# One one-hot compare, two maxima and four gelu buffers in a neighbour turn

## The reference

```python
y = affine(conv1x1(x, fc1_w, fc1_b), fc1_s, fc1_t)
nodes = window_partition(y, 8).reshape(Bw, C, 64).transpose(0, 2, 1)
idx = knn_idx(nodes, 9)                      # cosine distance, top_k
x_j = nodes[idx]; x_i = nodes[:, :, None, :]
feat = concatenate([x_i, x_j - x_i], -1)     # 2C
h = gelu((feat @ ew.T + eb) * es + et)       # 96 channels, exact gelu
h = max(h, axis=2)                           # over the 9 neighbours
x1 = affine(conv1x1(h, fc2_w, fc2_b), fc2_s, fc2_t) + x
```

## Time and profile before

| | |
|---|---|
| median of three runs | 654.57 us |
| span of the profiled execution (first to last instruction) | 650.4 us |
| what lies outside the span, against the median | 4.2 us |
| PE busy | 572.0 us, 88% |
| DVE busy | 500.3 us, 77% |
| ACT busy | 435.5 us, 67% |
| POOL busy | 249.4 us, 38% |
| maxima (L1221), 128 of 1203 ns | 151.7 us |
| one-hots (L1206), 64 of 766 ns | 48.9 us |

### The profile page before, as it was taken

The page is one execution under the profiler, slowest core; times in us unless marked ns, Lnnn a source line. Parts: engine busy times, 40 slices in busy tenths (PEclk is TensorE's granted clock), DMA queues, the critical chain, the costliest instruction groups (busy, mean ns, idle before and its releaser), DMA issues.

```text
span 650.4 us, 12840 instructions
## 1 busy us (share of the span) xinstructions
PE 572.0 (88%) x3404; PEld 339.7 (52%) x3404; DVE 500.3 (77%) x962; ACT 435.5 (67%) x645; POOL 249.4 (38%) x299
## 2 busy tenths in 40 slices
PE   6993699999999999939888899999999999988970
PEld 1232466666666556625545566666665565545530
DVE  2687679999999999947998666666667667655665
ACT  3761379999999999928877555555565655644545
POOL 2650103333333333304857534444444434433310
PEclk9995599999999999969989999999999999989985
DMA  8847655666566656685531222222112222296516
GB/s 218 264 144 213 173 137 132 142 147 146 138 147 145 143 145 139 147 164 127 116 71 36 52 62 50 49 50 51 42 33 59 80 75 80 57 182 128 128 54 194
DMA packets 101605, 75.76 MB, mean 116 GB/s; under 512 B 52738, under 2 KB 84996, under 8 KB 101236
## 3 DMA queue, kind: packets, MB, share of 16 engines
q1 hardware_dynamic: 100804, 71.69, 45.6%
q10 hardware_dynamic: 768, 3.67, 2.2%
HBM read 48.84 MB, written 22.15 MB: 109 GB/s over the span
## 4 chain that ended last, share of the span: by engine, by line
PE 40%; DVE 29%; issue 13%; SPq 6%; DMA 5%; ACT 3%; DVEq 1%; POOL 1%; ACTq 0%; POOLq 0%
DVE hmax L1221 12%; PE pz L703 9%; PE pz L682 7%; DVE onehot L1206 5%; PE pz L697 5%; PE p_edge L703 4%; DVE idx L1197 4%; PE p_edge L682 4%; PE pz L533 3%; PE p_edge L697 2%; DVE val L1189 2%; DMA y_hl<-y_d 2%; PE pz L611 2%; DMA ht<-xh 2%; PE p_keys L525 1%
## 5 line engine op out<-in xcount | busy, mean ns | idle before, releaser
L1221 DVE TENSOR_REDUCE hmax<-gel 96x128 f32<-96x1024 f32 x128 | 151.7, 1203 | 19.3 <-ACT gel L828 19.3
L828 ACT ACTIVATE gel<-pz 96x1024 f32<-96x1024 f32 x128 | 130.4, 1018 | 39.5 <-PE pz L611 27.0
L1098 POOL CAST ht<-h 48x512 fp32r<-48x512 f32 x62 | 37.5, 605 | 148.8 <-DVE h L1332 148.3
L703 PE MATMUL pz<-ht,w_xh 128*112 128x512 f32 x258 | 73.0, 419 | 6.1 <-DMA ht<-xh 6.1
L1100 POOL TENSOR_TENSOR ht<-h,ht 48x512 fp32r<-48x512 f32 x62 | 73.5, 1185 | 5.0
L682 PE MATMUL pz<-xh,w_xh 128*112 128x512 f32 (+1 forms) x258 | 69.5, 406 | 0.8 <-DVE w_xh L1231 0.8
L611 PE MATMUL pz<-onehot,ab_hi 64*96 64x512 f32 x256 | 59.9, 464 | 3.0 <-ACT gel L828 2.4
L703 PEld LDWEIGHTS pz<-ht,w_xh 128*112 128x112 f32 x258 | 42.4, 177 | 33.2 <-issue 19.3
L893 ACT ACTIVATE pz<-c 48x512 f32<-48x512 f32 x43 | 25.7, 597 | 47.9 <-DVE c L1325 47.9
L682 PEld LDWEIGHTS pz<-xh,w_xh 128*112 128x112 f32 x258 | 46.0, 179 | 17.4 <-issue 1.2
L1332 DVE SCALAR_TENSOR_TENSOR h<-tgo,pz 48x512 f32<-48x512 f32 x43 | 29.7, 690 | 30.2 <-ACT pz L893 30.2
(11 more groups left out here) (148 smaller groups left out, 1242.0 us busy)
## 6 DMA issues: line engine op xcount, KB each, us to landing
ib<-idx_d SPq DMA_DIRECT2D x64, 256.0 KB, 4.2
y_d<-y SPq DMA_DIRECT2D x32, 192.0 KB, 3.6
y_hl<-y_d SPq DMA_DIRECT2D x32, 192.0 KB, 4.0
hist_d<-h SPq DMA_DIRECT2D x62, 96.0 KB, 1.9
hp<-hist_d SPq DMA_DIRECT2D x30, 192.0 KB, 2.7
kr<-xn_d SPq DMA_DIRECT2D x32, 98.0 KB
xn_d<-x_in SPq DMA_DIRECT2D x32, 96.0 KB, 2.4
kl<-xn_d SPq DMA_DIRECT2D x32, 96.0 KB
```

The lines of the kernel that those rows point to most:

```text
L703: mm = pe.matmul(gate_banks(k, d)[m][0:TOP, :], w_xh[:, 1, d, m, t], moving(ht, slice(0, P), t), start=False, stop=(t == TAPS - 1))
L828: act.activation(gel[:, t % 2], pz[0:O, 2 * (t % 2):2 * (t % 2) + 2, :], ACT.Gelu) \
L1098: pool.tensor_copy(h_slots(ht, 0, d), columns(h2[0:C, d])).then_inc(S["h_top"], 1)
L1221: dve.tensor_reduce(dst, gel[:, t % 2].rearrange("p w (r c k) -> p w r c k", r=WS, k=KN), AX_X, ALU.max).then_inc(S["maxed"], 1)
```

## The change

DVE compares all 2048 columns of a group in one instruction, and takes one maximum over two gelus (2048 columns) in place of two. The buffer gel has four places, one for each gelu of a group, and gelu t now waits for the maximum over the same half of the group before. The counts that other engines wait for (onehots, maxed) go with this: one one-hot and two maxima to a group. On DVE the order within a turn changes too: the one-hot of the next group comes first, then the first maximum, both parts of the top-k, the second maximum and the self maximum.

```diff
--- before.py
+++ after.py
@@ -137,7 +137,7 @@
                 ab_lo = a("ab_lo", [P, 2, Q, 2, O], F32R)
                 val8 = a("val8", [P, Q, KN], F32)
                 idx = a("idx", [P, 2, Q, KN], U16)
-                gel = a("gel", [O, 2, 2, E8], F32)
+                gel = a("gel", [O, Q, 2, E8], F32)
                 selfg = a("selfg", [O, 2, GN], F32)
                 hmax = a("hmax", [O, 2, GN], F32)
                 ident = a("ident", [P, E8], F32R)
@@ -327,7 +327,7 @@
 
                 sp.wait_ge(S[f"idx_stored{b}"], n * 16 + 16)
                 if later(g, 2):
-                    sp.wait_ge(S["onehots"], g * 2 - 2)
+                    sp.wait_ge(S["onehots"], g - 1)
                 for s in range(2):
                     sp.dma_start(ib[HALF * s:HALF * s + HALF, b],
                                  idx_d[reg(g, 0, 1)].rearrange("o (t s) n k -> s o t (n k)", s=2)[s]
@@ -601,7 +601,7 @@
 
                 if t == 0:
                     pe.wait_ge(S["ab_low"], g + 1)
-                pe.wait_ge(S["onehots"], g * 2 + (t // 2 + 1))
+                pe.wait_ge(S["onehots"], g + 1)
                 if t > 1 or later(g):
                     pe.wait_ge(S["gelus"], g * 4 + (t - 1))
                 for n, (part, which, moving) in enumerate(((ab_hi, 1, onehot[:, b, t]), (ab_lo, 1, onehot[:, b, t]),
@@ -823,9 +823,9 @@
 
             def gelu(g, t):
                 act.wait_ge(S["z_done"], g * 4 + (t + 1))
-                if t >= 2 or later(g):
-                    act.wait_ge(S["maxed"], g * 4 + (t - 1))
-                act.activation(gel[:, t % 2], pz[0:O, 2 * (t % 2):2 * (t % 2) + 2, :], ACT.Gelu) \
+                if later(g):
+                    act.wait_ge(S["maxed"], g * 2 + (t // 2 - 1))
+                act.activation(gel[:, t], pz[0:O, 2 * (t % 2):2 * (t % 2) + 2, :], ACT.Gelu) \
                     .then_inc(S["gelus"], 1)
 
             def fc2_out(g, b, n):
@@ -1071,10 +1071,8 @@
 
                 on(-2, x1_cast)
                 if exists(nth(j, b, 1)[0]):
-                    pool.wait_ge(S["onehots"], nth(j, b, 1)[0] * 2 + 1)
+                    pool.wait_ge(S["onehots"], nth(j, b, 2)[0])
                 on(-2, x1_low_first)
-                if exists(nth(j, b, 1)[0]):
-                    pool.wait_ge(S["onehots"], nth(j, b, 2)[0] * 2)
                 on(-1, residual)
                 on(-2, x1_low_second)
                 if isinstance(j, int) and GROUPS - 6 <= nth(j, b, 0)[0] < GROUPS - 4:
@@ -1197,28 +1195,26 @@
                     ins = dve.max_index(idx[:, b, t], val8[:, t], keys_of[t])
                 ins.then_inc(S["topk_done"], 1)
 
-            def one_hot(g, b, n, half):
-
-                if half == 0:
-                    dve.wait_ge(S["idx_here"], g * 32 + 32)
-                    if later(g, 2):
-                        dve.wait_ge(S["z_done"], g * 4 - 4)
-                dve.tensor_scalar(onehot[:, b, 2 * half:2 * half + 2], ib[:, b, 2 * half:2 * half + 2],
-                                  jcol_sb[:, 0:1], None, ALU.is_equal).then_inc(S["onehots"], 1)
+            def one_hot(g, b, n):
+
+                dve.wait_ge(S["idx_here"], g * 32 + 32)
+                if later(g, 2):
+                    dve.wait_ge(S["z_done"], g * 4 - 4)
+                dve.tensor_scalar(onehot[:, b], ib[:, b], jcol_sb[:, 0:1], None, ALU.is_equal) \
+                    .then_inc(S["onehots"], 1)
 
             def self_max(g, b, n):
 
                 dve.wait_ge(S["self_gel"], g + 1)
-                dve.wait_ge(S["maxed"], g * 4 + 4)
+                dve.wait_ge(S["maxed"], g * 2 + 2)
                 dve.tensor_tensor(hmax[:, b], hmax[:, b], selfg[:, b], ALU.max).then_inc(S["self_maxed"], 1)
 
-            def maxima(g, b, n, t):
-                dve.wait_ge(S["gelus"], g * 4 + (t + 1))
-                if t == 0 and later(g, 2):
+            def maxima(g, b, n, h):
+                dve.wait_ge(S["gelus"], g * 4 + (2 * h + 2))
+                if h == 0 and later(g, 2):
                     dve.wait_ge(S["fc2_done"], g - 1)
-                dst = hmax[:, b, HG * (t // 2):HG * (t // 2) + HG] \
-                    .rearrange("p (r w c) -> p w r c", r=WS, c=WS)[:, 2 * (t % 2):2 * (t % 2) + 2]
-                dve.tensor_reduce(dst, gel[:, t % 2].rearrange("p w (r c k) -> p w r c k", r=WS, k=KN),
+                dst = hmax[:, b, HG * h:HG * h + HG].rearrange("p (r w c) -> p w r c", r=WS, c=WS)
+                dve.tensor_reduce(dst, gel[:, 2 * h:2 * h + 2].rearrange("p t w (r c k) -> p (t w) r c k", r=WS, k=KN),
                                   AX_X, ALU.max).then_inc(S["maxed"], 1)
 
             def scan_weights(g, part):
@@ -1248,18 +1244,14 @@
                     if exists(nth(j, b, k)[0]):
                         stage(*nth(j, b, k), *part)
 
+                on(1, one_hot)
                 maxima(*now, 0)
-                on(1, one_hot, 0)
                 on(3, topk, 0)
+                on(3, topk, 1)
                 if not exists(nth(j, b, 3)[0]):
                     scan_weights(now[0], 0)
+                    scan_weights(now[0], 1)
                 maxima(*now, 1)
-                on(1, one_hot, 1)
-                on(3, topk, 1)
-                if not exists(nth(j, b, 3)[0]):
-                    scan_weights(now[0], 1)
-                maxima(*now, 2)
-                maxima(*now, 3)
                 self_max(*now)
 
             for c in range(9):
@@ -1294,8 +1286,7 @@
             for c in range(8, 12):
                 normed(c)
             dve.wait_ge(S["masks_set"], 9)
-            for half in range(2):
-                one_hot(0, 0, 0, half)
+            one_hot(0, 0, 0)
             for c in range(12, CHUNKS):
                 normed(c)
             for part in range(2):
```

## The result

The kernel after takes 674.23 us (median of four runs, 671.28 to 677.19) beside 655.11 us for the kernel before (four runs, 654.16 to 655.85): ratio 1.032, 95% interval 1.0281 to 1.0358. That is slower, as forecast. The time is 3.7 us above the 670.5 predicted and inside the range. The profiled execution took 673.76 us with a span of 671.9, against a span of 650.4 before: +21.5, where the sum had +15.9. Part of that difference is the choice of execution: between the medians it is +19.1 (655.11 to 674.23). Ratios here compare fast runs alone, and two executions of the experiments are left out of them as slow: 654.47 us in e5, and 872.87 us in e12, where the mean granted clock was 0.557 in place of some 0.94.

A forecast was written before the change was run, and what follows sets the result against it. DVE was taken to bound the kernel before, at 7.96 us a turn; afterwards a ring through ACT, at 8.50. 1.05 + 12.4 + 1.05 + 1.5 - 0.1 = +15.9 gave span 666.3, time 670.5 us; range 662 to 679.

The forecast's parts named there:

- the sum: Predicted changes of all stretches added, from turn 0 to the start of the scan: +15.9 us on the span.
- The ring: Each turn: self maximum, self_gelu, gelu 1, first maximum, MAX8, search, second maximum, next self maximum; 8.50 us against 7.96.
- 1.05 + 12.4 + 1.05: Turn 0's exposed double maximum; turns 1 to 23 at 0.54 each; the exposed double maximum after turn 25's transfer wait.
- the transfer's wait in turn 25: PE's 10.5 us wait for a transfer queued behind the scan weights, taken to absorb the 0.54 of turn 24.
- Turns 26 to 30: Late turns: 44.7 us in place of 43.2, with a stretched one-hot, the weight pass and a cast; +1.5.
- the start of the scan: Weight pass ends 1 us later after the self maximum, the last maxima 0.25 sooner; taken as -0.1.
- A: Rival: merging pays if gelu 1 is done within 1.9 us of the self maximum's start; 7.72 a turn, 650; chance 0.07.
- B: Rival: no change to speak of, overlapping starts already hide the fixed parts; 7.97 us per turn, 655 to 657; chance 0.04.
- the shadow of the ring: DVE's wait for gelu 1 ahead of the first maximum; the one-hot lies in it, so its saving is worth nothing.
- C: Rival: the one-hot meets GpSimd's cast and stretches beyond the wait for gelu 1; 675 to 690 us; chance 0.07.
- D: Rival: PE's 0.7 us idle ahead of the keys lowers the clock each turn; 30 us more, 700; chance 0.04.
- The signs: Listed for DVE: maxima 2.27, period 8.5, gap 0.45 released by gelu, one-hot 1.3, MAX8 to search 0.77, busy 10 less.

The follow-up runs named there:

- e5: Kernel before with only the one-hots merged, at the place of the first half; 647.93 us, ratio 0.9906.
- e12: e11 with ACT's two x1_high copies moved from between self_gelu and gelu 2 to ahead of gelu 1; 648.43 us, ratio 0.9935.
- e1: Kernel after with gelu 1 put ahead of self_gelu on ACT; 656.77 us, ratio 1.0084.
- e2: Kernel after with MAX8 put ahead of the first maximum on DVE; 661.01 us, ratio 1.0139.
- e4: Kernel before with only the maxima merged and four gelu buffers, two one-hots and the old order on DVE; 705.08 us, ratio 1.0811.
- e10: e5 with the last two maxima of a turn merged and four gelu buffers; 656.3 us, ratio 1.0068.
- e3: Kernel after with the edits of both e1 and e2; 654.96 us, ratio 1.0042.
- e9: e3 with the last gather ahead of fc2 on PE and gelu 3 ahead of fc2_out on ACT; 651.71 us, ratio 0.998.
- e11: e9 with GpSimd's second subtraction put ahead of the residual; 652.45 us, ratio 0.9992.

## Why the prediction was right, and which sizes were off

**The mechanism was right, point by point.** The ring was named with its links, and e1, e2 and e4 each change one link by what it holds. Predicted and measured, from the start of the self maximum (200.97 in the timeline above):

| | predicted | measured |
|---|---|---|
| self_gelu | 0.78 | 0.78 |
| gelu 1 | 1.28 | 1.27 |
| first maximum | 2.34 | 2.41 |
| MAX8 | 4.54 | 4.61 |
| search | 5.31 | 5.46 |
| second maximum | 6.12 | 6.28 |
| next self maximum | 8.50 | 8.57 |

- The durations: maximum 2.27 us, one-hot 1.28 (1.3 predicted), DVE's gap 0.51 (0.45).
- Two steps of the ring were too short. From the end of gelu 1 to the maximum 0.12 us passed, where I had 0.04 from turn 25. From MAX8 to the search it was 0.85, the upper bound, where I had 0.77; the start-up row has a shorter wait than the turns (0.17 against 0.24). One step was too long: the self maximum starts 2.29 after the second maximum, not 2.38. It follows 0.03 us after the end of that maximum, where I had 0.11; in turns 29 and 30 of the same kernel it is 0.10, and what sets this gap no run shows. That leaves +0.07 a turn in this one and +0.08 in the mean.
- Up to turn 25 the shift is 16.6 against 1.05 + 12.4 + 1.05 = 14.5 predicted. Of the 2.1 missing, 1.15 are turn 0 (2.2 in place of 1.05) and 1.9 are 0.08 a turn over 23 turns; the transfer's wait in turn 25 took back 1.0 more than I had given it.
- Turn 0: PE's first wait for y_hl ended at 80.59 in place of 79.13, and the transfer had been issued 1.4 us later (77.88 in place of 76.52). The first double maximum of the turn starts at 76.61, so this trace alone does not separate the two. But in the other kernels the self maximum of turn 0 lies anywhere between 85.94 (e10) and 89.45 (e3), and e1, which has every edit of the change, has it at 86.23. e1's transfer was issued at 74.53. So I count this as variation of the start and not as a cost of the change.
- Turns 26 to 30: +2.15 (18.75 - 16.6), predicted +1.5.
- **The step that failed in sign is the start of the scan**: -0.1 predicted, +1.3 measured (20.06 - 18.75). I let DVE's last maxima decide. The rows show PE instead: the scan's first matmuls wait for the weight pass, which ends 4.41 us after the self maximum of turn 30 in place of 3.44 (predicted: 1 us later), and after the gaps they run at the lower clock. DVE then waited 1.32 us for them.
- The rest up to +21.5, 1.4 us, comes within the scan: the shift of DVE's rows creeps from 20.1 to 20.3 over its first 54 half steps and goes to 21.5 in the last ten. No run took this apart.

**The base.** The prediction put 4.2 us outside the span. The run of the kernel after shows 1.9 (673.76 less 671.9); by that, the other 2 us were the distance of one execution from the median. They stood on both sides of the sum. But they flatter the forecast: by the spans the sum is 5.6 us short (15.9 against 21.5), by the medians 3.7, because the profiled execution before was a fast one of its kind.

**The rivals.** A fell as the change is written, by its own test: gelu 1 is done 2.29 us after the self maximum's start, not 1.9. Its 7.72 us a turn seems to come true in e12 (7.67), but that is luck: the 7.72 holds 0.23 for MAX8 and search in a row, which e12 does not pay. Without it A's price is 7.96 - 0.47 = 7.49. The merging of three pairs saved 0.29 a turn, not 0.47, about 0.10 a merge in place of 0.158, since the overlap of two starts goes with the instruction. B's steps, which are net of that overlap, had it right: 7.97 less the 0.23, and less 0.09 for the gap ahead of the self maximum, is 7.65. The Trainium skill ("VectorE: DVE Perf Modes", section on the TRN2 errata) states a fixed latency per instruction that one large tile pays once and many small ones each. e5 and e12 agree with its direction, with 0.12 us a turn for the merged one-hot and 0.29 for all three; in the kernel after the gain lies in the shadow of the ring. B fell: 8.58 is not 7.97. C fell, and in an unexpected way: the cast meets the one-hot, and it is the cast that is stretched, 1.27 to 1.34 us in the turns in place of mostly 0.39 and 0.60; the one-hot takes 1.27 to 1.29. The cast feeds nothing that is late. D fell for this kernel: the clock is 1.00 from 90 to 275 us, though PE waits 0.98 us for the index search in each turn:

```profile
207.38 0.69 PE L559 MATMUL p_keys<-kr,kl 128*64 128x64 f32 x16 [0.98 <-DVE idx L1195]
```

The danger was real, though: in e4 the same kind of gap took the clock down in every sixth turn. In the late turns the clock fell in both kernels, to 0.50 from 328 to 330 before and from 355 to 358 after.

**The signs.** The maxima, the one-hot, the gap on DVE and its releaser, and the period came as listed. One sign did not: DVE's busy time was to fall by some 10 us, and it fell by 2.3 (500.3 to 498.0). In the turns it went from 98.6% of 7.96 to 90.6% of 8.58 us, 0.08 less a turn. Added durations would give 14.2; they count each overlap twice.

**Chances.** The time lies within the forecast's own range of 666 to 679. Redone from its terms, the ring behind that range goes from 8.31 to 8.78, not from 8.35 to 8.80, which moves it by about 1 us. The weight of 0.91 on slower rested on two rows, and the earlier trace rows, and they were enough.

## What to carry to other kernels

Before merging two instructions, ask when the later of their operands is ready, and what stands ahead of its producer in that engine's queue. Look at small waits on engines off the path: here one of 0.26 us was where the new path ran. When a merge loses, keep it and move the producers: the edits that brought 3.2% back, and 0.65% on top, removed no work at all.

## What the runs showed of the hardware

- MAX8 followed at once by the search on its values costs 0.24 to 0.25 us of waiting on the same engine, 0.85 us from start to start in place of 0.54 (e1); with a maximum between them nothing (e2).
- GpSimd's cast of 48x256 takes 1.27 to 1.34 us beside DVE's one-hot of 2048 columns, while the one-hot keeps its 1.28. Beside a maximum of 1024 columns it took mostly 0.39 and 0.60 in turn in the kernel before, and 0.39 and 1.10 in turn in e5, where its end reaches into the one-hot by 0.22 us; what sets these no run shows. The self maximum goes the other way: 0.69 us alone, 0.89 to 0.93 beside GpSimd's second subtraction (e9), and back to 0.69 when that is moved (e11).
- A PE gap of 0.98 us in every turn left the granted clock at 1.00 for 185 us. Two gaps in every turn, of some 1.0 and 0.75 us, brought it to 0.50 in every sixth turn (e4). Gaps of 1.72 and 2.13 us close together, with little PE work between, came with matmuls at the lower clock.
